# Spreading the norms, residual adds and transposes of a two-batch expert layer between the experts of the other batch

## The chip, the core and the metric

The kernel runs on one core of one Trainium2 chip. The metric is device time in microseconds (us). A core has five engines that each work through their own instruction list in order and meet only through semaphores: PE (TensorE, matmuls and transposes), DVE (VectorE), ACT (ScalarE), POOL (GpSimd) and SP (SyncE, which here only issues DMAs).

## What is computed

Two batches of 2048 rows of 256 values pass through one transformer layer:

```
x = x + layernorm(attention(layernorm(x)))      # 16 heads, relative position bias
h = layernorm(x)
gates = softmax(top-2 of (mean over rows of h) @ gate_w.T + gate_b)     # 8 gates for each batch
x = x + layernorm(sum over e of gates[e] * gelu(h @ expert_w[e].T + expert_b[e]))
```

All 8 experts are computed for every row, then weighted; six of the eight gates are zero.

## The kernel before

The attention is one loop over 8 pairs of heads with 8 slots each (2 batches by 4 chunks of 512 queries). It accumulates into `y` (32 tiles of 128 rows by 256, 16 tiles for each batch). The output product of each slot is added one slot later, so the last slot's part (`G_ALL`, the last chunk of batch 1) is finished after the loop: `den_s` goes by DMA to `den_c`, is inverted, comes back by DMA as `inv_r`, a product spreads it (`inverses`, L547), DVE normalises (L1036), ACT and DVE split the result into two f16 parts, two `output` products follow in one PSUM bank `pm`, and two `add_output` add them to `y` (L1053). Only then does the rest start.

SP loads `x` again (into `xr`, which lies over the attention's `qk`) and the expert weights (`ewf`, over `prob`) after these inverse DMAs. ACT and DVE split the weights into two f16 parts, `ewh` (L866) and `ewl` (L1152).

For each batch in turn, with TT = 16 tiles:

- DVE runs `statistics` of `y` (16 bn_stats L891, 16 bn_aggr L894, a square root on ACT L724, five small operations), `residual` (16 normalise rows L940, 16 adds L946), `statistics` of `xr`, and `normalise`: for each of 4 groups of 4 tiles, 4 rows L925 into one of two buffers, PE transposes (L459) into PSUM banks `st`, ACT copies the high f16 part (L732), DVE makes the low part (L915).
- the gate: DVE reduces `pooled`, PE multiplies by the gate weights (L695), DVE and ACT (an Exp, L872) form the softmax, PE spreads it over the partitions (L698), DVE copies it to `gate`.
- the experts: 4 chunks (t) of 16 units (m), so 64 units for each batch. A unit n is six matmuls (L713) into bank `n % 4` of `st`, a Gelu on ACT into one of 8 slots of a ring `ge` (L880), and a weighted sum on DVE into `accf[t % 2]` (L1196; L1201 for the first two units of a chunk). PE may run four units ahead of the Gelu. After chunk t's units, `back(b, t-1)` transposes the sums of the chunk before back to rows (L684), and DVE's `ft_copy` puts them into `y` (L1187).
- then `statistics` and `residual` once more, and one store of the batch's 16 tiles.

Batch 1's part before its experts begins when batch 0's last `residual` is done. The only Gelus, Exp and square roots after the loop stand in ACT's list as the code has them:

```
for b in range(B):
    ln_sqrt(B + 3 * b)
    ln_sqrt(B + 3 * b + 1)
    high_tokens(B + b)
    ...Exp of the gate...
    ...64 Gelus...
    ln_sqrt(B + 3 * b + 2)
```

Of the kernel before, what the change touches and what calls it, by code (L numbers as in the profile page):

```python
# [11 lines left out]
E = 8  # L12
# [56 lines left out]
LN_STEPS = 2 * TT + 7  # L69

# [34 lines left out]
def jobs_of(g):  # L105

    out = []
    for s, (kind, n) in sorted(JOBS.items()):
        if kind == "proj":
            if g % CHUNKS == CHUNKS - 1:  # L110
                continue
            n += 4 * (g % CHUNKS)
        out.append((s, kind, n))
    return out

# [25 lines left out]
def layer(nc, x, w_pairs, wo, rel_bias, gate_wT, gate_b, expert_wT, expert_bT, onehot, rows, eye, out, w_scratch, t_scratch):  # L141
# [4 lines left out]
    with ctx:  # L146
# [74 lines left out]
        xn = [a[:, :, :].rearrange("p h q -> p (h q)") for a in acc]  # L221
# [76 lines left out]
        gate_set = sem("gate_set")  # L298
        ff_ready = sem("ff_ready")
# [4 lines left out]
        out_done = sem("out_done")  # L304

# [27 lines left out]
        def _(sp):  # L333
# [65 lines left out]
            inverse_in(G_ALL)  # L399
# [6 lines left out]
            for b in range(B):  # L406
                sp.dma_start(xr[:, TT * b:TT * b + TT, :], x[b, :, :].rearrange("(t p) d -> p t d", p=128)).then_inc(xr_in[b], 16)
                if b == 0:
                    sp.dma_start(ewf, expert_wT.rearrange("(k p) n -> p k n", p=128)).then_inc(ew_in, 16)
            for b in range(B):  # L410
                sp.wait_ge(res, (2 * b + 2) * TT)
                sp.dma_start(out[b, :, :].rearrange("(t p) d -> p t d", p=128), xr[:, TT * b:TT * b + TT, :]).then_inc(out_done, 16)
            sp.wait_ge(out_done, 16 * B)
# [3 lines left out]
        def _(pool):  # L417
# [3 lines left out]
            pool.wait_ge(tr_ready, B * GROUPS)  # L421
# [26 lines left out]
        def _(pe):  # L448
            def transposes(k):

                for g in range(GROUPS):
# [5 lines left out]
                    for a in range(KT):  # L457
                        for t in range(4):
                            last = nc.tensor.transpose(st[:, 2 * (g % 2) + a, 128 * t:128 * t + 128],  # L459
                                                       xn[g % 2][:, D * t + 128 * a:D * t + 128 * a + 128], ident[:, :])  # L460
# [88 lines left out]
            def output(G, t, loads):  # L549
# [6 lines left out]
                for n in range(2):  # L556
# [3 lines left out]
                    for r, (o, w) in enumerate(terms):  # L560
                        last = nc.tensor.matmul(pm[:, D * n:D * n + D], o, w, start=(r == 0), stop=(r == len(terms) - 1))  # L561
# [108 lines left out]
            for t in range(YJ):  # L670
                if t:
                    pe.wait_ge(y_add, G_ALL * YJ + t + 1)
                output(G_ALL, t, None)
            pe.wait_ge(y_add, (G_ALL + 1) * YJ + 1)
# [13 lines left out]
            for b in range(B):  # L688
                if b:
                    pe.wait_ge(gelu_done, CHUNKS * FF * b)  # L690
                transposes(B + b)
# [4 lines left out]
                last.then_inc(g_log, 1)  # L696
                pe.wait_ge(gv, b * 11 + 11)
                nc.tensor.matmul(pm[:, 0:E], ones[0:1, :], g1[0:1, 7, :], start=True, stop=True).then_inc(g_bc, 1)  # L698

                pe.wait_ge(ew_hi, 1)  # L700
                pe.wait_ge(ew_lo, 1)
                pe.wait_ge(xh_a, (B + b + 1) * KT * GROUPS)
                pe.wait_ge(xl_v, (B + b + 1) * KT * GROUPS)
                for t in range(CHUNKS):
                    for m in range(FF):
                        n = (b * CHUNKS + t) * FF + m
                        if n >= 4:
                            pe.wait_ge(gelu_done, n - 3)
                        cols = slice(S * b + QC * t, S * b + QC * t + QC)
                        terms = [(w[:, k, 128 * m:128 * m + 128], a[:, k, cols]) for k in range(KT)  # L710
                                 for w, a in ((ewh, xh), (ewl, xh), (ewh, xl))]
                        for r, (w, a) in enumerate(terms):
                            last = nc.tensor.matmul(st[:, n % 4, :], w, a, start=(r == 0), stop=(r == len(terms) - 1))  # L713
                        last.then_inc(ff_ready, 1)
                    if t:
                        back(b, t - 1)
                back(b, CHUNKS - 1)
# [3 lines left out]
        def _(act):  # L721
# [139 lines left out]

            sums_of_psum(G_ALL)
            high_inverse(G_ALL)
            high_output(G_ALL)
            act.wait_ge(ew_in, 16)
            nc.scalar.activation(ewh, ewf, ACT.Copy, scale=W_UNIT).then_inc(ew_hi, 1)  # L866
            for b in range(B):
                ln_sqrt(B + 3 * b)
                ln_sqrt(B + 3 * b + 1)
                high_tokens(B + b)  # L870
                act.wait_ge(gv, b * 11 + 6)
                nc.scalar.activation(g1[0:1, 5, :], g1[0:1, 1, :], ACT.Exp, bias=g1[0:1, 4, 0:1]).then_inc(g_exp, 1)  # L872
                if b == 0:
                    act.wait_ge(ew_lo, 1)
                for m in range(CHUNKS * FF):
                    n = b * CHUNKS * FF + m
                    act.wait_ge(ff_ready, n + 1)
                    if n >= 8:
                        act.wait_ge(ff_acc, n - 7)
                    nc.scalar.activation(ge[:, n % 8, :], st[:, n % 4, :], ACT.Gelu, bias=eb[:, m % FF:m % FF + 1],  # L880
                                         scale=1.0 / W_UNIT).then_inc(gelu_done, 1)
                ln_sqrt(B + 3 * b + 2)
# [353 lines left out]
```

## Time and profile before

| | us |
|---|---|
| median of 3 runs | 3255.93 (3251.97 to 3259.44) |
| profiled execution, its own time | 3255.61 |
| its span (first to last instruction) | 3253.8 |
| PE busy | 2884.5 (89%) |
| DVE busy | 1946.7 (60%) |
| ACT busy | 1604.1 (49%) |
| POOL busy | 2273.1 (70%) |

Busy time is a mean over the whole span; the attention loop takes most of it (to about 2909 us), and the change touches only what comes after. There the same engines look quite different, so the stretches have to be read one by one.

### The profile page before, as it was taken

The numbers are of one execution on the slowest core, as the hardware profiler recorded it, in microseconds if no ns is written. First come the engines' busy times: TensorE is split into PE (matmuls) and PEld (weight loads), VectorE is DVE, ScalarE is ACT, GpSimd is POOL, SyncE is SP. The second block draws the span as 40 slices with busy tenths as digits, with TensorE's granted clock in tenths as the row PEclk, the third lists the DMA queues.
The fourth block names the chain that finished last, engine by engine and source line by source line (L and its number), as shares of the span: only waits on it lengthen the run. The fifth ranks groups of instructions, "written<-read, shape, count | busy, mean of one in ns | idle before, by whom it ended". The sixth has DMA issues, their size and how long they took to land.

```text
span 3253.8 us, 58126 instructions
## 1 busy us (share of the span) xinstructions
PE 2884.5 (89%) x18988; PEld 1074.2 (33%) x18988; DVE 1946.7 (60%) x4926; ACT 1604.1 (49%) x2048; POOL 2273.1 (70%) x1033
## 2 busy tenths in 40 slices
PE   3599999999999999998999999999999999974756
PEld 1133333333333333333333333333333333322323
DVE  5465656565556655655656565656566566546676
ACT  2255555555555455555555555555554555543333
POOL 0188888887888788888888888878887888860000
PEclk9699999999999999999999999999999999986878
DMA  6000000000000000000000000000000000010000
GB/s 154 17 1 2 1 6 14 2 1 1 19 1 2 1 19 1 1 2 18 1 2 1 7 13 2 1 1 19 1 1 1 18 2 1 2 49 30 1 26 26
DMA packets 45640, 38.30 MB, mean 12 GB/s; under 512 B 21318, under 2 KB 43846, under 8 KB 45046
## 3 DMA queue, kind: packets, MB, share of 16 engines
q1 hardware_dynamic: 45302, 34.13, 4.0%
q8 instruction: 171, 2.80, 0.4%
q14 instruction: 167, 1.37, 0.1%
HBM read 29.17 MB, written 11.34 MB: 12 GB/s over the span
## 4 chain that ended last, share of the span: by engine, by line
PE 60%; issue 18%; DVE 12%; ACT 6%; DMA 1%; SPq 1%; DVEq 0%; ACTq 0%; POOL 0%; POOLq 0%
PE po L531 20%; PE st L501 17%; PE pre L513 6%; PE st L713 5%; PE pm L469 4%; ACT prob L764 4%; PE pm L561 3%; DVE mpart L1006 3%; PE pm L475 2%; DVE st L1023 2%; DVE pre L1003 2%; PE pm L540 1%; ACT o L797 1%; ACT qk L745 1%; DMA t_scratch<-w_scratch 1%
## 5 line engine op out<-in xcount | busy, mean ns | idle before, releaser
L441 POOL TENSOR_TENSOR acc<-acc,prob 128x1024 f32<-128x1024 f32 x896 | 2112.8, 2358 | 478.8 <-ACT prob L764 438.1
L764 ACT ACTIVATE prob<-st 128x1024 f32<-128x1024 f32 x1026 | 1017.9, 1021 | 1042.7 <-DVE st L1023 733.3
L531 PE MATMUL po<-prob,v 128*64 128x512 f32 x4096 | 992.6, 605 | 0.0
L501 PE MATMUL st<-qk 64*128 64x512 f16 x6156 | 845.6, 381 | 19.3 <-ACT prob L764 16.5
L998 DVE CUSTOM_DVE_ANT_0 pre<-pre,ew 128x512 f32<-128x512 f32 x460 | 308.9, 713 | 611.5 <-issue 611.5
L1003 DVE CUSTOM_DVE_ANT_0 pre<-pre,tab 128x512 f32<-128x512 f32 x716 | 483.9, 716 | 111.5 <-issue 110.3
L501 PEld LDWEIGHTS st<-qk 64*128 64x128 f16 x6156 | 296.3, 95 | 346.7 <-ACT prob L764 56.2
L513 PE MATMUL pre<-qk 64*128 64x512 f16 x1630 | 318.6, 388 | 87.0 <-DVE mpart L1006 35.7
L501 PE MATMUL st<-eq,ek 64*128 64x512 f16 x2052 | 394.3, 381 | 0.0
L531 PEld LDWEIGHTS po<-prob,v 128*64 128x64 f32 x4096 | 248.6, 136 | 439.6 <-issue 369.7
L1006 DVE TENSOR_REDUCE mpart<-pre 128x2 f32<-128x1024 f32 x227 | 277.8, 1224 | 120.9 <-PE pre L513 117.6
L777 ACT ACTIVATE ew<-pre 128x1024 f32<-128x1024 f32 x230 | 233.6, 1016 | 96.3 <-PE pre L513 89.6
L1023 DVE TENSOR_TENSOR st<-st,t 128x512 f32<-128x512 f32 (+2 forms) x352 | 260.7, 741 | 0.0
L513 PEld LDWEIGHTS pre<-qk 64*128 64x128 f16 x1630 | 79.0, 94 | 467.1 <-issue 150.5
L441 POOL TENSOR_TENSOR acc<-prob 128x1024 f32<-128x1024 f32 x64 | 150.8, 2355 | 92.0 <-ACT prob L764 81.1
L984 DVE SCALAR_TENSOR_TENSOR qk<-pm,qk 128x512 f16<-128x512 f32 x128 | 88.2, 689 | 152.6 <-ACT qk L745 152.6
L713 PE MATMUL st<-xh,ew 128*128 128x512 f16 x512 | 154.9, 385 | 0.0
L513 PE MATMUL pre<-ew,qk 64*128 64x512 f16 x460 | 91.5, 395 | 58.9 <-DVE mpart L1003 37.6
L501 PEld LDWEIGHTS st<-eq,ek 64*128 64x128 f16 x2052 | 101.0, 95 | 124.4 <-issue 5.2
L459 PE MATMUL st<-ident,acc 128*128 128x128 f32 x128 | 28.6, 406 | 125.7 <-issue 91.1
L880 ACT ACTIVATE prob<-st,eb 128x512 f32<-128x512 f32 x128 | 87.9, 688 | 82.4 <-PE st L713 82.4
L1196 DVE SCALAR_TENSOR_TENSOR acc<-prob,gate,acc 128x512 f32<-128x512 f32 x112 | 84.2, 752 | 62.8 <-ACT prob L880 62.8
(142 smaller groups left out, 2466.5 us busy)
## 6 DMA issues: line engine op xcount, KB each, us to landing
t_scratch<-w_scratch SPq DMA_DIRECT2D x2, 3072.0 KB
inv_r<-inv SPq DMA_DIRECT2D x260, 1.0 KB, 1.7
y<-x SPq DMA_DIRECT2D x2, 2048.0 KB, 11.3
qk<-x SPq DMA_DIRECT2D x2, 2048.0 KB, 12.7
out<-qk SPq DMA_DIRECT2D x2, 2048.0 KB, 7.5
w<-w_pairs SPq DMA_DIRECT2D x9, 384.0 KB, 3.7
t2f<-t_scratch SPq DMA_DIRECT2D x9, 384.0 KB, 4.5
t<-t_scratch SPq DMA_DIRECT2D x8, 384.0 KB, 3.2
```

Source lines behind the costliest of these rows:

```text
L441: nc.gpsimd.tensor_tensor(acc[g % 2][:, :, :], a, prob[:, n % RING, :, :], ALU.add).then_inc(sum_p, 1)
L469: last = nc.tensor.matmul(bank, w, t, start=(n == 0), stop=(n == len(terms) - 1))
L501: last = nc.tensor.matmul(st[:, 2 * (n % 2) + h, :], w[64 * h:64 * h + 64, :], t[64 * h:64 * h + 64, :], start=(r == 0), stop=(r == len(te ...
L513: last = nc.tensor.matmul(pre[:, h, :], qh[b][64 * h:64 * h + 64, at:at + 128], keys[64 * h:64 * h + 64, :], start=True, stop=True)
L531: last = nc.tensor.matmul(po[64 * h:64 * h + 64, :], v[:, g // CHUNKS, j, 64 * h:64 * h + 64], prob[:, n % RING, h, :], start=(s == 0), st ...
L713: last = nc.tensor.matmul(st[:, n % 4, :], w, a, start=(r == 0), stop=(r == len(terms) - 1))
L764: nc.scalar.activation(prob[:, n % RING, :, :], st[:, 2 * (n % 2):2 * (n % 2) + 2, :], ACT.Exp).then_inc(exp_done, 1)
L777: nc.scalar.activation(twin[:, :, :], pre[:, :, :], ACT.Relu).then_inc(pre_used, 2)
L998: nc.vector.tensor_tensor_reduce(pre[:, h, :], pre[:, h, :], twin[:, h, :], 1.0, NEG, ALU.add, ALU.max, mpart[:, c, h, t, kc:kc + 1, 0]).t ...
L1003: nc.vector.tensor_tensor_reduce(pre[:, h, :], pre[:, h, :], tab[:, h, at:at + 4, :].rearrange("p n u -> p (n u)"), 1.0, NEG, ALU.add, ALU ...
L1006: nc.vector.reduce_max(mpart[:, c, :, t, kc, 0], pre[:, :, :], AX.X).then_inc(pre_used, 2)
L1023: nc.vector.tensor_tensor(o, o, t1[:, :, at:at + hi - lo], ALU.add).then_inc(band_in, 1)
```

## The change

After the loop the work is cut into smaller pieces and put at written places of the lists:

- **SP**: `x` of batch 0 and the expert weights are loaded before the last slot's inverse DMAs, `x` of batch 1 behind them. Batch 1 is stored in four chunks.
- **Norms**: eight instead of six: `LN_RES` (after attention), `LN_FF` (before the experts), `LN_OUT` (batch 0's last) and `LN_LAST` + c (batch 1's last, one for each chunk). Each has its own small tiles. `variances` and `deviations` are the DVE halves before and after ACT's `norm_sqrt`; deviations also forms -mean/std, so that ACT can write a normalised tile as one Identity with scale and bias from memory (`norm_in_place`, `norm_tokens`). DVE keeps one add for each 4 tiles (`add_rows`).
- **Batch 0 before the experts**: its residual norm starts at once after the loop, ahead of the last slot's inverse on both DVE and ACT. The last slot's two output products go to two banks, and their adds come behind batch 0's tokens.
- **The experts**: the gate product is placed after unit 11 of a batch's first chunk, the spread after unit 15, and DVE takes up the chunk's 16 sums only after that (ring `ge`: 16 slots instead of 8). Batch 1's residual, norm, tokens and transposes lie in batch 0's chunks 0 to 3; batch 0's last norm and adds in batch 1's chunks 0 and 1; batch 1's last norm by chunk in its chunks 1 to 3 and behind. `back` stands after unit 5 of the chunk that follows.
- `xn`, the rows to be transposed, has a buffer pair for each batch, over `v`; POOL's first memset no longer waits for the transposes.

The core of the diff, PE:

```diff
+            def expert(b, t, m):
+                n = at_unit(b, t, m)
+                if n >= 4:
+                    pe.wait_ge(gelu_done, n - 3)
+                elif n % 2 == 0:
+                    pe.wait_ge(xh_a, KT * (B * GROUPS + 3 + n // 2))
+                    pe.wait_ge(xl_v, KT * (B * GROUPS + 3 + n // 2))
...
+            transposes(B)
...
+                        expert(b, t, m)
+                        if (t, m) == (0, 11):
+                            gate_log(b)
+                        if (t, m) == (0, 15):
+                            gate_rows(b)
+                        if m == 5 and b * CHUNKS + t:
+                            back(b - (t == 0), (t - 1) % CHUNKS)
+                        if b == 0 and t == CHUNKS - 1 and m % 4 == 2:
+                            if m == 2:
+                                pe.wait_ge(gate_set, 1)
+                            spare_transposes(B + 1, m // 4)
+            back(B - 1, CHUNKS - 1)
```

ACT:

```diff
+            norm_sqrt(LN_RES[0])
             sums_of_psum(G_ALL)
+            for g in range(GROUPS):
+                norm_in_place(LN_RES[0], 0, 0, range(4 * g, 4 * g + 4)).then_inc(yn_set, 1)
             high_inverse(G_ALL)
-            high_output(G_ALL)
             act.wait_ge(ew_in, 16)
             nc.scalar.activation(ewh, ewf, ACT.Copy, scale=W_UNIT).then_inc(ew_hi, 1)
+            norm_sqrt(LN_FF[0])
+            high_output(G_ALL)
+            high_tokens(B)
+            norm_sqrt(LN_RES[1])
+            act.wait_ge(ew_lo, 1)
...
+                        if (b, t, m) == (0, 0, 0):
+                            for g in range(GROUPS):
+                                norm_in_place(LN_RES[1], 1, 0, range(4 * g, 4 * g + 4)).then_inc(yn_set, 1)
+                        if (t, m) == (0, 14):
+                            act.wait_ge(gv, b * 11 + 6)
+                            nc.scalar.activation(g1[0:1, 5, :], g1[0:1, 1, :], ACT.Exp, bias=g1[0:1, 4, 0:1]).then_inc(g_exp, 1)
+                        if (b, t, m) == (0, 2, 2):
+                            norm_sqrt(LN_FF[1])
+                        if (b, t) == (0, 2) and m in (8, 11):
+                            norm_tokens(B + 1, 1, m // 9)
...
+                        if (b, t, m) == (1, 1, 0):
+                            norm_sqrt(LN_OUT)
+                        if (b, t) == (1, 1) and m in (6, 8, 10, 12):
+                            g = (m - 6) // 2
+                            norm_in_place(LN_OUT, 0, 0, range(4 * g, 4 * g + 4)).then_inc(yn_set, 1)
+                        if b == 1 and t >= 1:
+                            c = t - 1
+                            if m == 11:
+                                norm_sqrt(LN_LAST + c)
+                            if m == 14:
+                                norm_in_place(LN_LAST + c, 1, 4 * c, range(4 * c, 4 * c + 4)).then_inc(yn_set, 1)
+                        act.wait_ge(ff_ready, n + 1)
+                        if n >= GE:
+                            act.wait_ge(ff_acc, n - GE + 1)
+                        nc.scalar.activation(ge[:, n % GE, :], st[:, n % 4, :], ACT.Gelu, bias=eb[:, m:m + 1],
+                                             scale=1.0 / W_UNIT).then_inc(gelu_done, 1)
```

DVE:

```diff
+            for n in range(TT):
+                tile_sums(LN_RES[0], n, y[:, n, :])
+            variances(LN_RES[0])
+            deviations(LN_RES[0])
             invert(G_ALL)
+            dve.wait_ge(xr_in[0], 16)
+            for g in range(GROUPS):
+                add_and_sum(0, g)
+            variances(LN_FF[0])
             normalise_output(G_ALL)
+            deviations(LN_FF[0])
             low_output(G_ALL)
+            for g in range(GROUPS):
+                tokens(0, g)
+                if g:
+                    low_tokens(B, g - 1)
+                if g == 1:
+                    dve.wait_ge(ew_hi, 1)
+                    nc.vector.scalar_tensor_tensor(ewl, ewf, W_UNIT, ewh, ALU.mult, ALU.subtract).then_inc(ew_lo, 1)
+            low_tokens(B, GROUPS - 1)
+            for t in range(YJ):
+                add_output(G_ALL, 0, t, (pm, po)[t])
+            dve.wait_ge(y_add, (G_ALL + 1) * YJ + 1)
+            pool_tokens(0)
+            for n in range(TT):
+                tile_sums(LN_RES[1], n, y[:, TT + n, :])
+            variances(LN_RES[1])
+            deviations(LN_RES[1])
+            gate_of(0)
...
+                        if (b, t, m) == (1, 0, 0):
+                            pool_tokens(1)
+                            gate_of(1)
+                        expert_sum(b, t, m)
+                        if m == 6 and b * CHUNKS + t:
+                            ft_copy(b - (t == 0), (t - 1) % CHUNKS)
+                        if (b, t) == (0, 1) and m in (4, 7, 10, 13):
+                            add_and_sum(1, (m - 4) // 3)
+                        if (b, t, m) == (0, 1, 15):
+                            variances(LN_FF[1])
+                        if (b, t, m) == (0, 2, 3):
+                            deviations(LN_FF[1])
+                        if (b, t) == (0, 3) and m % 4 == 3:
+                            low_spare(B + 1, m // 4)
+                        if (b, t) == (1, 0) and 8 <= m < 12:
+                            chunk_sums(0, m - 8)
+                        if (b, t, m) == (1, 0, 12):
+                            variances(LN_OUT)
+                        if (b, t, m) == (1, 1, 2):
+                            deviations(LN_OUT)
+                        if (b, t) == (1, 1) and m in (8, 10, 12, 14):
+                            add_rows(0, (m - 8) // 2, 2 * GROUPS + (m - 8) // 2 + 1)
+                        if b == 1 and t >= 1:
+                            if m == 7:
+                                chunk_sums(1, t - 1)
+                            if m == 9:
+                                variances(LN_LAST + t - 1)
+                            if m == 12:
+                                deviations(LN_LAST + t - 1)
+                            if m == 15:
+                                add_rows(1, t - 1, 3 * GROUPS + t)
```

What these call, where it is new: `add_and_sum` is `add_rows` (one add of 128x1024) and 4 bn_stats; `chunk_sums` is 4 bn_stats; `expert_sum` waits for `gelu_done` of its unit; `deviations` waits for ACT's square root; `back` waits for all 16 sums of its chunk (`ff_acc`).

## Rows read from the trace of the kernel before

**Rows 1.** Stages after the loop: stretch, length, busy of PE, PEld, DVE, ACT, POOL, clock, DMA.
```profile
2908.75:2981.55 72.80, 13.38 (x60) 8.98 (x57) 45.18 (x152) 13.99 (x26) 0.31 (x2) 0.53 0.25 87
2981.55:3071.84 90.29, 88.37 (x416) 41.44 (x416) 49.56 (x68) 46.47 (x66) 0.00 (x0) 0.98 0.00 1
3071.84:3135.55 63.71, 7.55 (x40) 6.40 (x40) 57.29 (x218) 8.58 (x22) 0.00 (x0) 0.54 0.10 33
3135.55:3225.66 90.11, 88.18 (x416) 41.42 (x416) 49.54 (x68) 45.30 (x65) 0.00 (x0) 0.98 0.00 1
3225.66:3253.80 28.14, 0.00 (x0) 0.00 (x0) 19.61 (x72) 0.22 (x1) 0.00 (x0) 0.53 0.22 75
```

**Rows 2.** The chain that ended last, first batch: start, us, what.
```profile
2978.47 0.00 DVE g L932
...
2979.73 0.31 ACT g L872
...
2980.96 0.59 PE pm L698 x2
...
3024.80 0.87 PE pre L684 x8
...
3047.27 20.73 PE st L713 x96
```

**Rows 3.** Timeline at the loop's end and at batch 0's first tokens.
```profile
2908.06 0.69 DVE L1053 SCALAR_TENSOR_TENSOR y<-pm,y 128x512 f32<-128x512 f32 x1
...
2909.43 0.60 ACT L782 ACTIVATE o_raw<-po 128x512 f32<-128x512 f32 x1 [1.66 <-PE po L531]
...
2965.16 2.67 DVE L925 TENSOR_SCALAR acc<-qk,mv,rstd 128x256 f32<-128x256 f32 x8
```

**Rows 4.** DMA issues of short stretches: KB each, us from issue to landing.
```profile
qk<-x SPq DMA_DIRECT2D x1, 2048.0 KB, 8.2
prob<-expert_wT SPq DMA_DIRECT2D x1, 2048.0 KB, 12.8
...
den_c<-den_s SPq DMA_DIRECT2D x2, 2.0 KB, 1.7
...
rb<-rel_bias SPq DMA_DIRECT2D x2, 2.0 KB, 6.4
...
out<-qk SPq DMA_DIRECT2D x1, 2048.0 KB, 7.5
```

**Rows 5.** Groups by line and shape, 2909 to 3254: busy us, mean ns, idle before.
```profile
L880 ACT ACTIVATE prob<-st,eb 128x512 f32<-128x512 f32 x128 | 87.9, 688 | 82.4 <-PE st L713 82.4
L1196 DVE SCALAR_TENSOR_TENSOR acc<-prob,gate,acc 128x512 f32<-128x512 f32 x112 | 84.2, 752 | 62.8 <-ACT prob L880 62.8
...
L1187 DVE COPY y<-pre 128x1024 f32<-128x1024 f32 x8 | 9.8, 1219 | 2.5 <-PE pre L684 2.5
...
L1201 DVE TENSOR_SCALAR acc<-prob,gate 128x512 f32<-128x512 f32 x16 | 7.8, 486 | 16.0 <-ACT prob L880 16.0
...
L1152 DVE SCALAR_TENSOR_TENSOR ew<-prob,ew 128x4096 f16<-128x4096 f32 x1 | 4.4, 4424 | 8.7 <-ACT ew L866 8.7
L724 ACT ACT_TABLE_LOAD x3 | 3.8, 1283 | 0.1
```

**Rows 6.** Timeline of the tail.
```profile
3226.95 5.32 DVE L891 BATCH_NORM_STATS2 stats<-y 128x6 f32<-128x256 f32 x16
3232.30 1.17 DVE L894 BATCH_NORM_AGGREGATE mv<-stats 128x2 f32<-128x6 f32 x16
...
3233.71 0.22 ACT L724 ACTIVATE std<-var 128x16 f32<-128x16 f32 x1 [9.89 <-DVE var L896]
...
3235.09 5.26 DVE L940 TENSOR_SCALAR y<-y,mv,rstd 128x256 f32<-128x256 f32 x16
...
3245.86 0.38 SPq L412 DMA_DIRECT2D out<-qk  x1
```

**Rows 7.** The first 3.45 us of batch 0's experts, columns as in Rows 1.
```profile
2981.55:2985.00 3.45, 3.45 (x9) 1.24 (x10) 0.17 (x1) 0.70 (x1) 0.00 (x0) 0.50 0.00 0
```

More of the change, by code:

```diff
@@ L69 @@
 LN_STEPS = 2 * TT + 7
+LN_RES = [2, 4]
+LN_FF = [3, 5]
+LN_OUT, LN_LAST = 6, 7
+LN_OPS = 6
+GE = 16
 JOBS = {1: ("den", 0), 2: ("proj", 0), 4: ("proj", 1), 6: ("proj", 2), 8: ("inv", 0), 11: ("max", 0), 12: ("y", 0), 14: ("y", 1),
@@ L114, in jobs_of, with ln_call, ln_tiles, at_unit @@
     return out
+def ln_call(k):
+    return TT if k < LN_LAST else TT // CHUNKS
+def ln_tiles(k):
+    return sum(ln_call(n) for n in range(B, k + 1))
+def at_unit(b, t, m):
+    return (b * CHUNKS + t) * FF + m
 def shape_tables():
@@ L547, in inverses, with output @@
                 nc.tensor.matmul(pm[:, :], sel[:, :], inv_r[:, :], start=True, stop=True).then_inc(inv_ready, 1)
-            def output(G, t, loads):
+            def output(G, t, loads, bank=pm):
                 if t == 0:
@@ L670, in _ @@
             for t in range(YJ):
[L671 to L674, printed above, removed]
+                output(G_ALL, t, None, (pm, po)[t])
             def back(b, t):
@@ L709, in _ @@
[L709 to L716, printed above, removed]
@@ L860, in _, with norm_sqrt, norm_tile, norm_in_place @@
                     rest(n + 1)
+            def norm_sqrt(k):
+                act.wait_ge(ln_add, k + 1)
+                _, _, rows_k = norm(k)
+                nc.scalar.activation(rows_k[:, 1, 0:ln_call(k)], rows_k[:, 0, 0:ln_call(k)], ACT.Sqrt).then_inc(ln_sq, 1)
+            def norm_tile(k, n, to, src):
+                _, _, rows_k = norm(k)
+                return nc.scalar.activation(to, src, ACT.Identity, bias=rows_k[:, 4, n:n + 1], scale=rows_k[:, 2, n:n + 1])
+            def norm_in_place(k, b, first, tiles):
+                act.wait_ge(e_inv, LN_OPS * (k - B + 1))
+                for n in tiles:
+                    last = norm_tile(k, n - first, y[:, TT * b + n, :], y[:, TT * b + n, :])
+                return last
@@ L885, in _ @@
+            c = CHUNKS - 1
+            norm_sqrt(LN_LAST + c)
+            norm_in_place(LN_LAST + c, 1, 4 * c, range(4 * c, 4 * c + 4)).then_inc(yn_set, 1)
         @block.vector
@@ L1145, in _, with tile_sums @@
                     rest(n + 1)
-            invert(G_ALL)
-            normalise_output(G_ALL)
-            low_output(G_ALL)
-            for t in range(YJ):
-                add_output(G_ALL, 0, t)
-            dve.wait_ge(ew_hi, 1)
-            nc.vector.scalar_tensor_tensor(ewl, ewf, W_UNIT, ewh, ALU.mult, ALU.subtract).then_inc(ew_lo, 1)
-            dve.wait_ge(y_add, (G_ALL + 1) * YJ + 1)
-            for b in range(B):
-                statistics(B + 3 * b, y, b)
-                residual(B + 3 * b, 2 * b, b)
-                statistics(B + 3 * b + 1, xr, b)
-                normalise(B + b, B + 3 * b + 1, xr, b)
+            def tile_sums(k, n, src):
+                sums, _, _ = norm(k)
+                nc.vector.bn_stats(sums[:, n, :], src).then_inc(e_stat, 1)
@@ new lines, in add_rows, with add_and_sum @@
+            def add_rows(b, g, done):
+                at = TT * b + 4 * g
+                dve.wait_ge(yn_set, done)
+                to = xr[:, at:at + 4, :].rearrange("p t d -> p (t d)")
+                nc.vector.tensor_tensor(to, to, y[:, at:at + 4, :].rearrange("p t d -> p (t d)"), ALU.add).then_inc(res, 1)
+            def add_and_sum(b, g):
+                add_rows(b, g, b * GROUPS + g + 1)
+                dve.wait_ge(res, b * GROUPS + g + 1)
+                for t in range(4):
+                    tile_sums(LN_FF[b], 4 * g + t, xr[:, TT * b + 4 * g + t, :])
@@ new lines, in tokens @@
+            def tokens(b, g):
+                _, means, rows_k = norm(LN_FF[b])
+                k = B + b
+                if g >= 2:
+                    dve.wait_ge(tr_ready, k * GROUPS + g - 1)
+                for t in range(4):
+                    n = 4 * g + t
+                    last = nc.vector.tensor_scalar(xn[b][:, g % 2, D * t:D * t + D], xr[:, TT * b + n, :], means[:, n, 0:1],
+                                                   rows_k[:, 2, n:n + 1], ALU.subtract, ALU.mult)
+                last.then_inc(xn_ready, 1)
@@ L1210 @@
+            c = CHUNKS - 1
+            ft_copy(B - 1, c)
+            chunk_sums(1, c)
+            variances(LN_LAST + c)
+            deviations(LN_LAST + c)
+            add_rows(1, c, 3 * GROUPS + c + 1)
 def kernel(L0_attn_hidden_states, L0_attn_wq, L0_attn_wk, L0_attn_wv, L0_attn_wo, L0_attn_rel_bias,
```

189 lines of the change are left out of this document (125 added, 64 removed).

## The prediction

> **What bounds the kernel now.** I read the page first: attention to about 2909 us, where PE is busy throughout, and the change leaves that loop alone. Then the table of stages [rows 1] for what follows; it adds to 345 us. In the two expert stages (90.3 and 90.1 us) PE is busy for 88 and the clock is 0.98, so PE bounds them; DVE and ACT are half idle there. In the other three (72.8, 63.7 and 28.1 us) PE has little or nothing to do, DVE is at work for 45, 57 and 20, and the clock is 0.53. So 164.6 us are DVE's chains, with PE waiting. The chain of waits [rows 2] gives the unit of the expert stage: 16 units in 20.73, 1.295 us each, and a transposition back 0.87.
>
> **How I go about the change.** It adds no large work. It moves operations in lists that are worked through in order, and so the question is what stands in front of what. I walk the four lists from the loop's end with durations from rows; each time below is on the span's scale of the profiled execution.
>
> Prices first. 16 bn_stats take 5.3, one tile's 0.33; 16 bn_aggr with the add 1.4; the square root 0.2 [rows 6]; the six small operations of `deviations` 1.3 to 1.4 (five of them lie between the root at 3233.71 and the first normalise row at 3235.09, [rows 6], and a sixth of 0.2). A weighted sum lasts 0.752, the first two of a chunk 0.49 [rows 5]; with sums waiting in line they follow closer, as bn_stats do (0.33 apart), so I take 0.68, with 0.752 as the upper bound: a chunk of 16 is 10.4. The 1024-wide add isn't in the trace; the copy of that width takes 1.22 [rows 5], so with four bn_stats a group is 2.6. A table load is 1.28 [rows 5], a Gelu 0.69.
>
> An Identity of 128x256 with scale and bias from memory isn't there either. The 512-wide Gelu takes 0.69 and the 16-wide root 0.22 [rows 5, 6]; halfway between is 0.45. Half of 0.69 (0.35) is the lower bound, 0.69 the upper; the second operand costs something, so 0.47, nearer the low end: 7.5 for 16 tiles, 1.9 for 4.
>
> **Front, to the first unit.** DVE leaves the loop at 2908.75 [rows 3]. Batch 0's rows of `y` are complete (the last slot belongs to batch 1), so its norm runs at once: 5.3 + 1.4 + 0.2 + 1.3, to 2917.1. But ACT's list now has this root before `sums_of_psum`, so `den_s` is written at 2916.5, some 6 later than before. SP meanwhile issues `x` and the expert weights at about 2909.5, when the last product is over [rows 3]. They land after 8.2 and 12.8 [rows 4], at 2917.7 and 2922.8, where before they were issued at 2917. The small `den_c` transfer is then behind 4 MB. Such a transfer takes 1.7 on an empty queue, but 6.4 at the start, behind the two loads of `x` [rows 4]; so I let it land at 2923.1, against 2918.8 were it not held. DVE stands at `invert` until then: that wait is new. After it, four groups of 2.6 (ACT's Identities are ahead of them), and 1.4: 2935.2. The inverse product is ready by then, since ACT's 16 Identities end at 2924.7 and what follows is short: two 16-wide copies, four transfers of the kind that takes 1.7 [rows 4], one product. Then L1036 0.7, deviations 1.3, low half 0.7: 2938.0. Tokens and transposes took 13.3 before (2965.16 to 2978.47, [rows 2, 3]); now `ewl` is among them (4.4, [rows 5]) and PE comes 1.5 late from the output products: to 2957.2. Unit 0 needs only three of the four groups: **2955.3**, against 2981.55.
>
> **The first Gelu.** That gain of 26 is not kept. Units 0 to 3 fill the four banks (5.2, and 1.7 for the half clock of the first 3.45 us, [rows 7]): 2962.2. ACT's next entries are batch 1's root and 16 Identities, and the root waits for DVE: after 2957.2 two output adds 1.4, pooled 0.3, 5.3 + 1.4 + 0.2 + 1.3, to 2967.1; 16 Identities 7.5; load 1.3; Gelu 0.7. So unit 4 starts at 2976.7: PE waits 14.5, again in a cold state (1.7).
>
> **Batch 0's chunks.** Units 4 to 15 take 15.5 + 1.7. The gate's Exp stands before Gelu 14, with a load ahead of it; the Exp and what follows it to PE take 0.3 and 0.9 [rows 2]: PE waits about 1.0 after unit 15, to 2995.2. Only now DVE can begin the 16 sums: 3005.8, and PE is at `back` after unit 21 at 3003.0: wait 2.8. Chunk 1's sums with four groups and the copy are 10.4 + 10.4 + 1.2 = 22.0: 3027.8, PE there at 3027.4: 0.4. `norm_sqrt(LN_FF[1])` stands before Gelu 34 and waits for `variances` (3029.2); root, load back and Gelu 2.2: unit 38 starts at 3031.4, PE having been ready at 3028.7: wait 2.7. After that neither ACT (8 Identities in a chunk of 20.7, beside Gelus of 10) nor DVE holds PE. 26 units, one back and four spare transpositions at 0.87: batch 0 ends at **3069.5**, with no 63.7 stage behind it.
>
> **Batch 1's chunks.** DVE enters `gate_of(1)` at once and waits there for PE's product behind unit 75, so it does nothing for 15 us while 16 Gelus pile up (exactly the ring). PE is past the gate at 3092.1, the wait 0.8. DVE then owes, before `variances(LN_OUT)` is done, 13 sums 8.5, a copy 1.2, 16 bn_stats 5.4 and 1.4: 3108.8. ACT's root for it stands before Gelu 80: 0.2 + 1.3 + 0.7, 3111.0. PE had used up its four banks at 3097.3: **wait 13.7**, and 1.7 cold. Chunk 1 holds 20 Identities (9.4), two loads, a root and 16 Gelus, 22 on ACT against 21.6 on PE, and Gelu 94 waits behind DVE's third add and `deviations`: I walk it to 5.6 of waits; the next chunk 0.4. 44 units 57.0, three backs 2.7, cold 1.7, waits 6.0: 3178.4.
>
> **Tail.** Four Identities and a root stand before the last Gelus, so Gelu 127 ends 3.7 late: 3182.1. Sum 0.75, batch 1's third add 1.2 (the transposition beside it), copy 1.2, bn_stats 1.4, aggregates 0.6, root 0.2, deviations 1.3, Identities 1.9, add 1.2: 3191.9. The store is a quarter of one that took 7.5; 1.7 of it fixed [rows 4], so 3.2, and 0.5 to the end: **3195.6**. Before, the store began at 3245.86 [rows 6].
>
> The span goes from 3253.8 to 3195.6, by 58.2. The profiled execution's own time is 3255.61, 0.3 below the median; 3255.9 - 58.2 gives 3197.7, say **3198**.
>
> Of a table switch the rows say 1.28 for the load. The Trainium skill (ScalarE: Activation LUTs, What ACT_TABLE_LOAD costs) has the same load and a drain of 1.38 on top, 2.66 for a switch. By the row the sum is as above; by the page, ten exposed switches (the second rival says which) would add 14, an estimate from that page: 3212.
>
> **Rivals.**
>
> *The lists don't collide* (0.11). In favour: DVE and ACT have 40 us of idle time in each expert stage, more than the moved work. Against: four banks give PE about 4 us of freedom, and the waits at units 4 and 84 are for work that is serial on DVE. Without the waits (14.5, 1.0, 2.8, 0.4, 2.7, 0.8, 13.7, 6.0 and 1.7 of clock, 43.6) the time is 3154.
>
> *A table switch costs more than its load* (0.08). By the lists there are 17 loads after the loop where there were 7 (the three of L724 in [rows 5], and an Exp and a Gelu for each batch), ten of the switches before a Gelu or Exp for which PE waits in turn. Were each to cost its load again, 1.28, the time is 3211. The same Trainium skill page speaks for this one; before, no switch was long enough exposed to tell.
>
> *ACT binds batch 1's later chunks* (0.07). If an Identity takes 0.69, chunk 1 needs 26 on ACT, the first Gelu is 3.5 later, the tail 0.9: with about 4 more in each of two chunks, 3211. Against it: only chunk 1 has more than eight Identities.
>
> *Slower: PE loses its clock* (0.03). PE now has nine waits instead of one long one. If they keep the grant at half, each unit costs 1.295 more; from 45 units on the gain is gone, and with all 128 the time is 3364. In favour: wherever PE worked sparsely the clock was 0.53 [rows 1]. Against: full clock came after 3.45 of steady work [rows 7], and between waits stand runs of 15 units and more.
>
> No change at all: 0.01, since nothing here takes 58 back without one of these.
>
> **Range.** The forecast has 0.70. Its bounds: `den_c` not held back -4, Identity at 0.35 -3, no second cold start -3.4: 3187; upwards three short waits with a cold start each +5, Identity at 0.69 +6, sums at 0.752 +3: 3212, which takes in the two rivals at 3211. So 3187 to 3212. The measurement can tell about 0.2% (6.5 us) from no change. Faster 0.96, same 0.01, slower 0.03.
>
> **What would show it.** After: `den_c` lands near 2923; PE's first L713-like product near 2955, a gap of 14 behind four units; a gap of 3 behind unit 21; nothing idle near 3070; a gap of about 14 behind the 84th unit, ended by a Gelu behind a root; last store issued near 3192. Identity near 0.47 to 0.57. It is wrong if DVE's wait at the second gate isn't there, or if the gaps are filled: then towards 3154; wrong upwards if loads or Identities are dearer.

## The result, and the profile after

The changed kernel takes 3198.94 us (3198.38 to 3199.48, 4 runs), the kernel before in the same comparison 3256.05: a ratio of 0.9825, interval 0.9808 to 0.9842, 57 us less. Forecast were 3198 and a range of 3187 to 3212.

The profiled execution has a span of 3197.7. Its loop ends at 2910.91, where before it ended at 2908.75 [rows 3]. That is not the change's doing: in the executions below the loop's end lies anywhere from 2906.8 to 2913.4, with the same loop, and 1.6 of the 2.2 are there before its first Exp. So I measure from the loop's end (in the changed kernels, the start of DVE's first instruction behind it). After it the kernel before takes 345.05, the changed one 286.79, 58.3 less; the forecast said 58.2.

The table of stages of the changed kernel, columns as in [rows 1]; first in three parts, then the middle part cut at its waits:

```profile
2910.91:2955.69 44.78, 10.57 (x54) 7.45 (x50) 34.95 (x109) 18.66 (x36) 0.44 (x2) 0.63 0.41 141
2955.69:3179.76 224.07, 184.89 (x869) 86.80 (x867) 142.44 (x339) 137.36 (x225) 0.00 (x0) 0.93 0.04 15
3179.76:3197.70 17.94, 1.97 (x8) 1.57 (x8) 8.87 (x23) 6.78 (x12) 0.00 (x0) 0.56 0.17 59
...
2953.90:2977.60 23.70, 7.56 (x32) 4.06 (x32) 11.69 (x47) 12.15 (x28) 0.00 (x0) 0.72 0.00 0
...
3092.60:3111.00 18.40, 5.41 (x26) 2.30 (x25) 17.91 (x51) 4.82 (x8) 0.00 (x0) 0.79 0.00 1
3111.00:3138.30 27.30, 22.43 (x92) 9.92 (x92) 17.79 (x39) 21.20 (x39) 0.00 (x0) 0.89 0.00 1
3138.30:3179.50 41.20, 40.69 (x196) 19.24 (x196) 30.72 (x64) 27.49 (x42) 0.00 (x0) 1.00 0.23 77
```

Set beside [rows 1]: the stretch to the first unit went from 72.8 to 44.8. The two expert stages and the one between them, 244.1 together, are now one of 224.1. The tail went from 28.1 to 17.9. The middle could have been shorter: PE is busy for only 185 of its 224. In 3092.60 to 3111.00 it is PE that idles and DVE that is full (17.9 of 18.4), the opposite of what an expert stage looked like before.

The timeline of PE in the changed kernel from the first unit on, only those instructions in front of which it sat idle for more than 0.3 us, with the idle time and what ended it in brackets:

```profile
2977.73 1.03 PE L753 MATMUL st<-xh,ew 128*128 128x512 f16 x2 [16.25 <-ACT prob L996]
2995.75 0.38 PE L740 MATMUL pm<-g,ones 1*128 1x8 f32 x2 [0.69 <-DVE g L1350]
3006.59 1.10 PE L716 MATMUL pre<-ident,acc 128*128 128x128 f32 x8 [2.58 <-DVE acc L1361]
3031.58 0.61 PE L753 MATMUL st<-xh,ew 128*128 128x512 f16 x2 [0.61 <-ACT prob L996]
3092.34 0.38 PE L740 MATMUL pm<-g,ones 1*128 1x8 f32 x2 [0.68 <-DVE g L1350]
3111.07 1.03 PE L753 MATMUL st<-xh,ew 128*128 128x512 f16 x2 [13.06 <-ACT prob L996]
3130.16 0.60 PE L753 MATMUL st<-xh,ew 128*128 128x512 f16 x2 [0.88 <-ACT prob L996]
3132.78 0.59 PE L753 MATMUL st<-xh,ew 128*128 128x512 f16 x2 [1.15 <-ACT prob L996]
3138.38 0.60 PE L753 MATMUL st<-xh,ew 128*128 128x512 f16 x2 [2.84 <-ACT prob L996]
3160.58 0.60 PE L753 MATMUL st<-xh,ew 128*128 128x512 f16 x2 [0.44 <-ACT prob L996]
3184.23 1.97 PE L716 MATMUL pre<-ident,acc 128*128 128x128 f32 x8 [4.47 <-DVE acc L1361]
```

The waits are 16.3 at unit 4, 13.1 at unit 84, and nine of 0.4 to 4.5. The bracket names ACT's Gelu for most of them, but a Gelu is only the last step. What stood in front of it shows in the same timeline on the other engines:

```profile
2918.40 1.21 SPq L406 DMA_DIRECT2D den_c<-den_s  x2
...
2925.49 0.24 DVE L1147 RECIPROCAL inv_c<-den_c 64x16 f32<-64x16 f32 x1 [6.27 <-DMA den_c<-den_s]
...
2967.71 7.97 ACT L927 ACTIVATE y<-y,tab 128x256 f32<-128x256 f32 x16 [1.43 <-DVE tab L1294]
2975.69 1.28 ACT L996 ACT_TABLE_LOAD   x1
2976.99 2.42 ACT L996 ACTIVATE prob<-st,eb 128x512 f32<-128x512 f32 x4
...
3086.41 0.15 DVE L1335 SCALAR_TENSOR_TENSOR g<-pm,g 1x8 f32<-1x8 f32 x1 [13.79 <-PE pm L735]
...
3108.80 0.22 ACT L923 ACTIVATE tab<-tab 128x16 f32<-128x16 f32 x1 [13.52 <-DVE tab L1275]
3109.04 1.28 ACT L996 ACT_TABLE_LOAD   x1
```

The last three are one story: DVE stood for 13.8 at batch 1's gate, owed the work afterwards, and ACT stood for 13.5 at the root that needed it.

### The profile page after: what moved, and what is told of

Same layout as the page of the kernel before. It is cut to its first block, busy times and chain, and to the rows that moved or that the text cites. A ratio compares the mean times of both kernels' runs of the same rounds, so it can differ in the third digit from the quotient of the medians.

```text
span 3197.7 us, 58114 instructions
## 1 busy us (share of the span) xinstructions
PE 2884.7 (90%) x18988; PEld 1071.6 (34%) x18988; DVE 1911.7 (60%) x4817; ACT 1651.9 (52%) x2141; POOL 2272.7 (71%) x1033
## 4 chain that ended last, share of the span: by engine, by line
PE 59%; issue 16%; DVE 14%; ACT 8%; DMA 1%; SPq 1%; DVEq 1%; ACTq 0%
PE po L566 20%; PE st L536 17%; PE pre L548 6%; PE pm L504 4%; ACT prob L822 4%; PE st L753 3%; PE pm L596 3%; DVE mpart L1124 3%; PE pm L510 3%; DVE st L1141 2%; DVE pre L1121 2%; PE pm L575 1%; ACT o L855 1%; ACT qk L803 1%; DMA t_scratch<-w_scratch 1%
## 5 line engine op out<-in xcount | busy, mean ns | idle before, releaser
L596 PE MATMUL pm<-wo,o 128*128 128x256 f16 x774 | 107.6, 275 | 7.3 <-DVE o L1159 7.3
L753 PE MATMUL st<-xl,ew 128*128 128x512 f16 x256 | 99.3, 388 | 0.0
```

The costliest lines, as they stand in the source:

```text
L596: last = nc.tensor.matmul(bank[:, D * n:D * n + D], o, w, start=(r == 0), stop=(r == len(terms) - 1))
```

## The experiments

Eleven runs were made: nine edited kernels, the changed kernel once more, and one of the nine once more. Times are medians. late_root, early_gate, spread_norm and den_first had only the kernel before beside them; changed_again, all_three, no_switch and one_store ran together, and in that set the changed kernel, the yardstick, takes 3197.25. Lengths "after the loop" are those of the profiled execution, from the loop's end; they leave out the loop's own scatter of some 6 us. Half clock below means a granted clock of 0.50 (1.2 of 2.4 GHz) while PE works. All edits are to the changed kernel, the last two on top of three others.

### The changed kernel again

> The changed kernel once more, unedited, as the yardstick beside the next three: about 3199 us. Every theory expects the same waits as in its first profile, since the lists are the same; what the TensorE clock does in the waits may differ by a few us between executions.

3197.25 us (3193.32 to 3201.37), ratio 0.9815, interval 0.9801 to 0.9828; after the loop 287.05 against 286.79. The eleven waits come again in the same places and within 0.02 us of the same lengths. They belong to the lists, not to chance.

### Is the root's place or DVE's backlog the cause of the wait at unit 84?

```diff
-                        if (b, t, m) == (1, 1, 0):
+                        if (b, t, m) == (1, 1, 5):
                             norm_sqrt(LN_OUT)
```

> Only ACT's root for batch 0's last norm moves, from before Gelu 80 to before Gelu 85 of the changed kernel. Theory (DVE's backlog from the second gate is the cause, the root only where it first shows): units 84 and 85 run early, but the transposition back behind unit 85 still waits for 16 sums that DVE finishes near 3111 on the changed kernel's scale, so a wait of about 10 us moves from unit 84 to the transposition and the time falls by 3 to 5 us, to about 3195. Rival (the root's place in ACT's list is the cause): the 13 us wait goes altogether and the time falls by 13 or more, to 3186 or less.

3197.56 us, ratio 0.981 (0.9794 to 0.9826). The timeline of PE:

```profile
3113.55 1.97 PE L716 MATMUL pre<-ident,acc 128*128 128x128 f32 x8 [10.20 <-DVE acc L1361]
```

Units 84 and 85 ran, and the transposition back waited 10.2 for DVE's sums instead: the backlog is the cause, and the root only showed it first. From batch 1's gate spread to the end it took 102.4 against 105.4, the 3 us that the theory gave. The whole time, expected near 3195, doesn't show them: up to that gate this execution took 3.6 longer, with stretches at half clock that the changed kernel's doesn't have (behind unit 4 for 5 us instead of 3, and behind the wait at unit 38).

The second edit moves batch 1's gate:

```diff
-                        if (t, m) == (0, 11):
+                        if (t, m) == (0, (11, 1)[b]):
                             gate_log(b)
-                        if (t, m) == (0, 15):
+                        if (t, m) == (0, (15, 6)[b]):
                             gate_rows(b)
...
-                        if (t, m) == (0, 14):
+                        if (t, m) == (0, (14, 4)[b]):
                             act.wait_ge(gv, b * 11 + 6)
```

> Batch 1's gate product stands behind its second unit instead of its twelfth, its Exp before Gelu 68 and its spread behind unit 70. Theory: DVE begins batch 1's sums near 3079 instead of 3093, so the wait of 13.1 us at unit 84 shrinks to 1 to 2, the half clock behind it (about 3 us) goes and the gate's wait of 0.7 too: 16 us less than the changed kernel, about 3183. Rival (DVE has too much work in these chunks, wherever it begins): the wait comes back at the transposition or at unit 84 with more than 5 us, and less than 9 us are won.

3186.09 us (3184.21 to 3192.1), ratio 0.9776 (0.9759 to 0.9792): 11 to 13 us less than the changed kernel's two medians, 13 to 16 by the ratios. The wait at unit 84 is 1.4, as expected. The profiled execution is the slowest of the four and only 9.5 shorter after the loop; 2.3 of what is missing is there before unit 38, where the lists are still the same. Its timeline and table of stages:

```profile
3105.09 0.61 PE L753 MATMUL st<-xh,ew 128*128 128x512 f16 x2 [1.40 <-ACT prob L996]
```

```profile
3129.50:3132.90 3.40, 3.40 (x9) 1.19 (x10) 3.40 (x4) 2.29 (x4) 0.00 (x0) 0.51 0.16 55
3105.10:3121.20 16.10, 15.28 (x74) 7.25 (x74) 13.29 (x29) 15.26 (x27) 0.00 (x0) 1.00 0.00 1
```

The second line is the stretch behind that wait, at full clock. But behind the 2.84 wait of this chunk (the first line) PE has half clock for 3.4 although it works without a break, which the changed kernel's execution did not have there. So the mechanism is as forecast, and a part of the gain depends on what the clock does after each remaining wait. The time is 3 above the expected 3183.

### The first Gelu

```diff
-            norm_sqrt(LN_RES[1])
             act.wait_ge(ew_lo, 1)
...
-                        if (b, t, m) == (0, 0, 0):
-                            for g in range(GROUPS):
+                        if (b, t, m) == (0, 0, 8):
+                            norm_sqrt(LN_RES[1])
+                        if b == 0 and t * FF + m in (9, 11, 16, 18):
+                            g = (9, 11, 16, 18).index(t * FF + m)
                             norm_in_place(LN_RES[1], 1, 0, range(4 * g, 4 * g + 4)).then_inc(yn_set, 1)
```

> Batch 1's first root stands before Gelu 8 and its 16 Identities in four groups before Gelus 9, 11, 16 and 18, instead of all before Gelu 0. Theory: the 16.3 us wait at unit 4 goes, waits of together 2 to 5 us appear around units 13 to 16 since two more table loads and the Identities share ACT with the Gelus: 12 to 15 us less than the changed kernel, about 3185. Rival (the first Gelu was late for DVE's or PE's sake): less than 5 us.

3183.1 us (3181.78 to 3184.62), ratio 0.977 (0.9754 to 0.9786); after the loop 272.6, 14.2 less. The wait at unit 4 is gone, and of those expected in its place there is one worth naming, at the gate (timeline of PE; a second is 0.35):

```profile
2977.01 0.38 PE L740 MATMUL pm<-g,ones 1*128 1x8 f32 x2 [2.17 <-DVE g L1351]
```

### The transfer of the denominators

The weights' load is issued inside the last `inverse_in`, right behind the two `den_c` transfers:

```diff
-            sp.dma_start(ewf, expert_wT.rearrange("(k p) n -> p k n", p=128)).then_inc(ew_in, 16)
-            inverse_in(G_ALL)
+            inverse_in(G_ALL, True)
```

> The weights' load of 2 MB is issued behind the two small transfers of the denominators instead of ahead of them; nothing else moves. Theory (the small transfer is held by the loads issued before it): it lands near 1 to 2.5 us after its issue instead of 6.5, DVE's wait at the inverse falls from 6.3 to about 2, and the first unit and all behind it come 4 us earlier, 3195. Rival (the transfer is slow for its own small pieces or for busy memory): its landing and the time stay within 1 us.

3192.52 us (3190.7 to 3195.65), ratio 0.98 (0.9782 to 0.9817); after the loop 282.95, 3.8 less. DMA issues of the changed kernel, then of this one, and this one's timeline:

```profile
den_c<-den_s SPq DMA_DIRECT2D x2, 2.0 KB, 6.6
```

```profile
den_c<-den_s SPq DMA_DIRECT2D x2, 2.0 KB, 1.7
```

```profile
2916.69 0.24 DVE L1148 RECIPROCAL inv_c<-den_c 64x16 f32<-64x16 f32 x1 [1.54 <-DMA den_c<-den_s]
```

The same transfer takes 6.6 behind the loads and 1.7 ahead of the second one. It lands 4.7 earlier after the loop's end; 4.0 of that reach unit 4; part of the rest is that DVE's first add now waits 0.4 for ACT's Identities. The Trainium skill (DMA: Bandwidth & Descriptors, Queues, rings and completion order) says that each DMA engine takes a queue's descriptors in the order of its ring; these rows agree with that but don't prove it. While the transfer was under way the 16 DMA engines were 91% busy in the changed kernel (2918.40 to 2925.20) and 52% here (2914.33 to 2916.20), so crowding as such, which the expectation put on the rival's side, would be undone by this edit too. Shown is that the loads ahead of it hold the transfer, and what moving one of them behind it gives.

### What a table switch costs

```diff
-                nc.scalar.activation(rows_k[:, 1, 0:ln_call(k)], rows_k[:, 0, 0:ln_call(k)], ACT.Sqrt).then_inc(ln_sq, 1)
+                nc.scalar.activation(rows_k[:, 1, 0:ln_call(k)], rows_k[:, 0, 0:ln_call(k)],
+                                     ACT.Copy if k in (LN_FF[1], LN_OUT) or LN_LAST <= k < LN_LAST + CHUNKS - 1 else ACT.Sqrt).then_inc(ln_sq, 1)
```

> Five roots inside the expert stage (the second of batch 1, batch 0's last, three of batch 1's last) are copies, so ten table loads go; the outputs are then not normalised rightly, everything else is in place. Theory (a switch costs its load of 1.28 and nothing more): the waits at units 38 and 112 go, that at unit 84 falls by 1.3, those in units 94 to 98 by some 2.6: 4 to 6 us less than the changed kernel. Rival (a drain of 1.4 more for each switch that PE waits for): 10 us or more less.

3195.55 us (3190.53 to 3196.67), ratio 0.9806 against 0.9815 of the changed kernel beside it. By the medians that is 1.7 less, short of the 4 to 6 expected and inside the scatter of the two kernels' runs; after the loop it is 281.4, 5.6 less than the 287.05 of the changed kernel's second profile. The rival's 10 or more is out by both. Timeline of PE and ACT:

```profile
3110.60 0.22 ACT L923 ACTIVATE tab<-tab 128x16 f32<-128x16 f32 x1 [14.82 <-DVE tab L1276]
3110.73 2.40 ACT L997 ACTIVATE prob<-st,eb 128x512 f32<-128x512 f32 x4
...
3111.45 1.03 PE L753 MATMUL st<-xh,ew 128*128 128x512 f16 x2 [11.64 <-ACT prob L997]
```

With the switch, 1.53 lie between the root's start and the Gelu's (3108.80 and 3110.33, where the load ends); without it 0.13. The wait at unit 84 falls by 1.4 (13.06 to 11.64), those of units 94 to 98 from 4.9 to 2.8, the one at the last transposition from 4.5 to 2.9, and the one at unit 112 goes. The one at unit 38, which was to go, is 0.9 where it was 0.6: PE had no half clock in front of it this time and came early. Unit 38 itself starts 23.6 behind the transposition after unit 21, against 25.0 in changed_again and in late_root, so there too 1.4 were won. At units 38 and 84, where one switch stands alone, that is the load of 1.28 and 0.1 more, not 2.66. (The changed kernel has nine norms, not eight as the section on the change says: ACT's root L923 stands in its trace 5 times with 16 columns and 4 times with 4. Its loads after the loop are the 17 of the prediction.) The Trainium skill (ScalarE: Activation LUTs, What ACT_TABLE_LOAD costs) has 2.66 for a switch; here the load starts 0.01 after the Identity before it ends (2975.68), the Gelu 1.30 after the load does (2975.69 and 2976.99 above), and the measurement decides.

### One store or four

```diff
-            for t in range(CHUNKS):
-                sp.wait_ge(res, 3 * GROUPS + t + 1)
-                sp.dma_start(out[1, QC * t:QC * t + QC, :].rearrange("(t p) d -> p t d", p=128),
-                             xr[:, TT + 4 * t:TT + 4 * t + 4, :]).then_inc(out_done, 16)
-            sp.wait_ge(out_done, 16 * (1 + CHUNKS))
+            sp.wait_ge(res, 4 * GROUPS)
+            sp.dma_start(out[1, :, :].rearrange("(t p) d -> p t d", p=128), xr[:, TT:2 * TT, :]).then_inc(out_done, 16)
+            sp.wait_ge(out_done, 16 * B)
```

> Batch 1 is stored in one transfer of 2 MB at the end instead of four of 512 KB. Theory (a store of 2 MB takes 7.5 us, one of 512 KB 3.2): 4 to 5 us more than the changed kernel. Rival (the last small store is held by the earlier ones or has a large fixed part): less than 2 us more.

3204.31 us (3201.24 to 3206.76), ratio 0.9838 (0.9825 to 0.9852), 7.1 above the yardstick by the medians; after the loop 291.65, 4.6 more than 287.05, with the same waits. The term of the sum was 4.3. The profiles don't say where the other 2.5 between the medians come from.

### The three edits together

> The three edits that each removed a wait together (weights' load behind the denominators' transfers, batch 1's first norm spread over Gelus 8 to 18, batch 1's gate early). Theory (the waits are separate collisions in the lists and add up): 4 + 15 + 13 to 16, 32 to 35 us less than the changed kernel, 3164 to 3167. Rival (one is the next one's cover, DVE or ACT becomes the bound): less than 25 us.

3164.68 us (3162.32 to 3165.71), ratio 0.9715 (0.9702 to 0.9728): 32.6 less than the yardstick, and no version of this case is faster. Run again with the next one it took 3163.63, ratio 0.9719; after the loop the two take 251.8 and 251.7. Its longest waits in the timeline of PE:

```profile
3077.36 0.60 PE L754 MATMUL st<-xh,ew 128*128 128x512 f16 x2 [1.41 <-ACT prob L998]
...
3101.75 0.60 PE L754 MATMUL st<-xh,ew 128*128 128x512 f16 x2 [2.84 <-ACT prob L998]
...
3147.61 1.12 PE L717 MATMUL pre<-ident,acc 128*128 128x128 f32 x8 [4.48 <-DVE acc L1363]
```

The collisions add up, as separate ones do: by the medians the three edits alone won 4.7, 14.2 and 11.2 against 3197.25, 30 together. After the loop the three together are 35.0 shorter, but alone they were 3.8, 14.2 and 9.5, or 27.5. The waits from the first unit to the end fall from 43.7 to 16.9 and unit 0 begins 3.9 earlier, together 30.6. The other 4 are time at half clock, which has nearly gone here: from unit 0 to the last transposition it is left at unit 0's start and behind one wait, that of the gate, for some 3 us, in both profiles.

> The three edits together once more, as the yardstick beside the version above: about 3165 us.

### Moving the rest earlier: a miss

Besides the three edits, five places change; the core:

```diff
-                        if (b, t) == (1, 1) and m in (6, 8, 10, 12):
-                            g = (m - 6) // 2
+                        if (b, t) == (1, 1) and m in (3, 5, 7, 9):
+                            g = (m - 3) // 2
...
-                            if m == 11:
+                            if m == 10:
                                 norm_sqrt(LN_LAST + c)
-                            if m == 14:
+                            if m == 12:
```

> The three edits together, and the places of five more steps: batch 1's second root before Gelu 37 instead of 34 and its deviations with it, batch 0's last Identities before Gelus 83, 85, 87, 89 instead of 86 to 92 with the adds behind them, and each of batch 1's chunk norms two to three units earlier. Theory (the waits left, 2.3 at unit 38, 4.9 in units 94 to 98 and 4.5 at the last transposition, are again only collisions): 2.3 + 3 + 3, about 8 us less than the three edits alone, 3157. Rival (ACT's work in that chunk, 22 us against PE's 21.6, is too much in any order): units 83 to 98 keep 4 us or more of waits and less than 5 us are won.

3170.62 us (3166.79 to 3173.23), ratio 0.9738: 7.0 more than the three edits alone, where 8 less were expected; after the loop 257.2, 5.5 more. Timeline of PE and ACT in batch 1's chunk 1:

```profile
3098.30 0.61 PE L754 MATMUL st<-xh,ew 128*128 128x512 f16 x2 [2.52 <-ACT prob L998]
3104.07 1.01 PE L754 MATMUL st<-xh,ew 128*128 128x512 f16 x2 [3.00 <-ACT prob L998]
...
3101.28 2.07 ACT L928 ACTIVATE y<-y,tab 128x256 f32<-128x256 f32 x4 [2.46 <-DVE tab L1296]
```

The waits in that chunk are 1.4, 0.9, three of 0.35, 2.5 and 3.0 against 1.4, 0.9, 1.2 and 2.8. Elsewhere the one behind batch 1's second root falls from 2.3 to 1.4, chunk 2's rises from 0.4 to 1.2 and the last transposition's from 4.5 to 5.0, so that all waits together grow by 2.9. Earlier Identities and roots only come sooner to the point where they wait for DVE, and behind them the Gelus wait too. Half clock after the last of these waits (1.01 for two matmuls, not 0.6) costs some more. The rival's number came true, but its reason, too much work in any order, is not shown by this run; the next one asks for it.

### Half of batch 0's last rows a chunk later

```diff
-                        if (b, t) == (1, 1) and m in (6, 8, 10, 12):
-                            g = (m - 6) // 2
+                        if (t, m) in ((1, 6), (1, 9), (2, 3), (2, 6)) and b:
+                            g = ((1, 6), (1, 9), (2, 3), (2, 6)).index((t, m))
...
-                        if (b, t) == (1, 1) and m in (8, 10, 12, 14):
-                            add_rows(0, (m - 8) // 2, 2 * GROUPS + (m - 8) // 2 + 1)
+                        if (t, m) in ((1, 8), (1, 11), (2, 5), (2, 8)) and b:
+                            g = ((1, 8), (1, 11), (2, 5), (2, 8)).index((t, m))
+                            add_rows(0, g, 2 * GROUPS + g + 1 + (g >= 2))
```

Not shown: batch 0's store now follows batch 1's first quarter, and the counts that the stores wait for change with it.

> The three edits together, and of batch 0's last 16 Identities and four adds only half in batch 1's chunk 1 (before Gelus 86 and 89), the other half in chunk 2 (before Gelus 99 and 102); all else where it was. Theory (chunk 1 simply holds too much: 22 us of ACT's work against 21.6 of PE's, with DVE full as well): the waits of 4.9 us in units 94 to 98 fall to 1 or less, chunk 2 gets none of more than 1: 3 to 4 us less than the three edits alone, about 3160. Rival (the waits come from the chain root, deviations, Identities of the chunk norm itself, whatever else is there): 3 us or more of waits stay around unit 98 and the time stays within 2 us.

3166.98 us (3166.17 to 3168.04), ratio 0.9715 (0.9702 to 0.9728), the same ratio as the three edits alone, where 3 to 4 us less were expected; after the loop 250.7, 1.0 less. Timeline of PE and ACT:

```profile
3104.00 0.60 PE L755 MATMUL st<-xh,ew 128*128 128x512 f16 x2 [2.28 <-ACT prob L999]
...
3101.30 2.07 ACT L929 ACTIVATE y<-y,tab 128x256 f32<-128x256 f32 x4 [2.54 <-DVE tab L1297]
```

Theory and rival had half each. The waits of 4.9 fall to 2.3, so half of them was load; the other half is the chain of the chunk norm itself, in which ACT waits 2.5 for DVE's deviations while Gelus stand behind it. Chunk 2's wait rises from 0.4 to 1.1.

## Why the prediction was right, point by point

**Front.** Unit 0 begins 44.8 after the loop's end, forecast 46.6. The denominators' transfer behind 4 MB, its landing (14.6 after the loop's end, forecast 14.4) and DVE's wait for it are as told, and den_first shows the price: 3.8, forecast 4.3 by the two landings. Of the 1.8 that the forecast is late, 0.4 are there when the last slot's low half is made (2939.76), 1.0 come with the tokens and transpositions (18.2, to 2957.94, for 19.2), and 0.4 in how far unit 0 runs ahead of the last token.

**The first Gelu.** Wait 16.3 for 14.5. Unit 4 begins 66.8 after the loop's end, forecast 68.0: the front was earlier, full clock came within the first unit (0.70 from 2956 to 2957, then 1.00) so that the four units took 5.8 and not 6.9, and DVE's chain behind them was as long as told (9.8 for 9.9). spread_norm confirms it by undoing it.

**The Identity.** 16 in 7.97, 0.50 each; I took 0.47 between bounds of 0.35 and 0.69. The 1024-wide add with its bn_stats is 2.56 a group for 2.6. Fourteen sums in line take 9.36, 0.67 each for 0.68.

**Batch 0's chunks.** Waits 0.7, 2.6 and 0.6 for 1.0, 2.8, 0.4 and 2.7; the 0.4 at the second transposition back is in none of the runs. The missing 2.1 at unit 38 are mostly no error of DVE's time: after the 2.6 wait PE ran some 3 us at half clock (0.50 from 3008 to 3010) that I had not charged there, and so came later to the Gelu. In late_root that stretch is absent, the wait is 2.3, and unit 38 starts 25.0 behind the transposition in both, forecast 25.6. Batch 0 ends without a gap; the 63.7 stage is gone.

**Batch 1's chunks.** The 13.8 of DVE's idle time at the second gate (forecast 15), the backlog, and the wait of 13.1 at unit 84 (13.7) came as walked; late_root and early_gate show the order of cause. Behind the wait the half clock lasted longer than I charged: in the table of stages of the changed kernel,

```profile
3103.40:3117.10 13.70, 6.03 (x17) 2.80 (x18) 11.40 (x42) 5.29 (x9) 0.00 (x0) 0.50 0.00 0
```

6.0 of these 13.7 lie behind the restart at 3111.07, which costs 3.0 for my 1.7. Chunk 1's waits are 4.9 for 5.6, chunk 2's 0.4 for 0.4. That units 94 to 98 wait for load and chain alike was only settled by tuned and two_chunks.

**Tail.** From unit 127's end 17.9, forecast 17.2. Here 4.5 of it are the wait of the last transposition (timeline of DVE and ACT):

```profile
3180.08 2.07 ACT L927 ACTIVATE y<-y,tab 128x256 f32<-128x256 f32 x4 [1.40 <-DVE tab L1294]
...
3191.00 2.07 ACT L927 ACTIVATE y<-y,tab 128x256 f32<-128x256 f32 x4 [1.24 <-DVE tab L1294]
```

The Identities at 3180.08 are those of the chunk before, in front of Gelus 126 and 127.

**The rivals.** That the lists don't collide would have given 3154; the changed kernel has 43.7 of waits from its first unit on, and 3164 is what the three undone collisions give. The dearer switch fell with no_switch. ACT as the bound of the later chunks is true only of chunk 1, and there by half (its price in the prediction, 3.5, 0.9 and 8, adds to 3210, not 3211). The clock went down for a few us after some waits and never stayed down.

**How much of it is luck.** The mechanism and the order of the waits came as told; that the total came within 1 us is in part luck. Counted from the loop's end, unit 0 came 1.8 before its forecast, unit 38 2.0, unit 84 2.1, unit 127's end 0.8 and the end of the span 0.1. So the front and the waits were forecast 2 too long, and the half clock behind unit 84 (1.3) and the tail (0.7) too short by as much.

## What to carry to other kernels

When work is spread among in-order lists, walk every list to its next wait before counting what is hidden: here the moved work fitted by busy time (half of DVE and ACT was free), and 44 us were still lost, 29 of them at two places, where a small instruction with a late input stood in front of many with ready ones. Put the instruction that others wait for where its input is ready, put the product that lets a whole backlog begin (the gate here) as early as its data allow, and issue a small transfer on a critical chain ahead of large loads; these three moves gave 33 us more. Placing everything earlier is not the same: in tuned it put the waiting instructions in front of more ready ones and lost 7.

## What the runs showed of the hardware that was not expected

Short waits differ in what they do to the clock. The wait of 2.84 us in batch 1's chunk 1 left full clock in the changed kernel and was followed by some 3.4 us at half clock in early_gate and in den_first (0.50 from 3130 to 3132), with the same instructions around it. The wait of 2.58 at the first transposition back was followed by half clock in the changed kernel and not in late_root. So profiled executions whose lists are equal up to a point differ by up to 3.6 us there, where the waits themselves mostly repeat within 0.02. What decides it stays open. The two kernels that were profiled twice had half clock in the same places both times, and agreed within 0.3 after the loop (286.79 and 287.05, 251.77 and 251.72).
